# Stages of a graph attention kernel that end on a barrier of semaphores alone, with two stages' semaphores cleared together

## The reference

```python
for l in range(2):
    q, k, v = x @ Wq[l] + bq[l], x @ Wk[l] + bk[l], x @ Wv[l] + bv[l]     # each as (2500, 8, 64)
    a = (q[dst] * k[src]).sum(-1) * scale                                 # scores, (40000, 8)
    e = exp(a - segment_max(a, dst)[dst])
    alpha = e / (segment_sum(e, dst)[dst] + 1e-16)
    agg = segment_sum(alpha * v[src], dst)
    x = agg + (x @ Ws[l] + bs[l]) + enc
x = layer_norm(x)
x = layer_norm(relu(x @ W1 + b1) @ W2 + b2 + x)
return outer_layer_norm(x_in + x + enc)
```

## Time and profile before

| | us |
|---|---|
| median of 3 runs | 2167.22 |
| lowest and highest | 2167.22, 2171.39 |
| span of the profiled execution (first to last instruction) | 2163.2 |
| first collecting stage, start of its first VectorE operation | 566.59 |
| second collecting stage, the same | 1470.65 |
| start of `finish`, the same | 1889.98 |

### The profile page before, as it was taken

The page is one execution under the profiler, slowest core; times in us unless marked ns, Lnnn a source line. Parts: engine busy times, 40 slices in busy tenths (PEclk is TensorE's granted clock), DMA queues, the critical chain, the costliest instruction groups (busy, mean ns, idle before and its releaser), DMA issues. The chain is left out here.

```text
span 2163.2 us, 31856 instructions
## 1 busy us (share of the span) xinstructions
PE 1834.1 (85%) x7461; PEld 1388.8 (64%) x7462; DVE 1881.0 (87%) x2308; ACT 696.3 (32%) x1748; POOL 1447.3 (67%) x1428
## 2 busy tenths in 40 slices
PE   6778999998389999996899999974988877779997
PEld 5656666666267787774666666653766655557876
DVE  7659999999789999884899999996999988878894
ACT  3223333333265555552233333323111111132222
POOL 3067777777667777774677777775777777657653
PEclk9889999999599999998899999986999999979999
DMA  7589889888668888885788988885777777641111
GB/s 285 186 269 292 277 285 290 273 284 276 207 202 261 266 258 263 265 261 208 253 272 278 291 280 278 288 264 161 211 210 210 211 210 210 185 164 59 59 49 47
DMA packets 194709, 492.05 MB, mean 227 GB/s; under 512 B 36555, under 2 KB 57931, under 8 KB 194646
## 3 DMA queue, kind: packets, MB, share of 16 engines
q0 software_dynamic: 106624, 349.00, 52.9%
q1 hardware_dynamic: 85142, 137.07, 18.1%
q10 hardware_dynamic: 2880, 5.24, 0.7%
HBM read 431.21 MB, written 59.66 MB: 227 GB/s over the span
## 5 line engine op out<-in xcount | busy, mean ns | idle before, releaser
L845 POOL DMA_INDIRECT all_work<-k_rows,all_work x664 | 630.3, 949 | 227.1 <-issue 189.7
L845 POOL DMA_INDIRECT v_ring<-v_rows,coll_index x632 | 615.4, 974 | 215.5 <-issue 198.2
L1490 PE MATMUL coll_banks<-coll_ev,coll_hot 128*128 128x260 f32 x2656 | 646.9, 392 | 85.8 <-DVE coll_ev L1586 44.8
L1490 PEld LDWEIGHTS coll_banks<-coll_ev,coll_hot 128*128 128x128 f32 x2656 | 491.6, 192 | 220.8 <-DVE coll_ev L1586 104.5
L1048 PE MATMUL score_q_ps<-score_q,score_hot 128*128 x1328 | 394.3, 422 | 84.5 <-DVE score_q L1088 54.4
L1076 DVE TENSOR_TENSOR all_work<-score_q_ps,all_work 128x1024 f32<-128x1024 f32 x332 | 404.6, 1220 | 44.6 <-PE score_q_ps L1048 18.7
L1586 DVE TENSOR_TENSOR coll_ev<-v_ring,coll_banks 128x1024 f32<-128x1024 f32 x332 | 402.5, 1213 | 37.6 <-DMA v_ring<-v_rows,coll_index 32.2
L1081 DVE TENSOR_REDUCE graph_edge<-all_work 128x1024 f32 (+1 forms) x332 | 397.9, 1209 | 0.0
L1048 PEld LDWEIGHTS score_q_ps<-score_q,score_hot 128*128 128x128 f32 x1328 | 258.1, 200 | 177.7 <-issue 125.8
L1157 ACT ACTIVATE score_hot<-score_local,all_iota_col 128x512 fp32r<-128x512 uint8 x166 | 119.9, 723 | 589.8 <-DVE all_work L1076 557.0
L1600 DVE TENSOR_TENSOR all_work<-all_work,coll_banks 128x520 f32 x354 | 244.2, 690 | 25.7 <-PE coll_banks L1490 19.1
(11 more groups left out here) (312 smaller groups left out, 2348.9 us busy)
## 6 DMA issues: line engine op xcount, KB each, us to landing
score_xt<-x_turned SPq DMA_DIRECT2D x42, 512.0 KB, 5.9
all_work<-k_rows,all_work POOLq DMA_INDIRECT x664, 4.6
score_local<-local_dst SPq DMA_DIRECT2D x166, 64.0 KB, 6.0
x_turned<-keys_xt SPq DMA_DIRECT2D x20, 512.0 KB, 4.4
score_skip<-in_x SPq DMA_DIRECT2D x40, 256.0 KB, 4.8
v_rows<-score_v_out SPq DMA_DIRECT2D x40, 256.0 KB, 5.2
skip_rows<-score_skip SPq DMA_DIRECT2D x40, 256.0 KB, 3.8
x_turned<-coll_xt SPq DMA_DIRECT2D x20, 512.0 KB, 4.3
```

What stands on the lines that cost most here:

```text
L845: nc.gpsimd.indirect_dma_start(rows[:, slot, t, :], None, table, at).then_inc(arrived[slot], 16)
L1490: last = nc.tensor.matmul(sums[sum_slots[u]][:, part, :], m, ev[:, s % EVS, t, part * AGG // 2:(part + 1) * AGG // 2], start=s == 0 or t = ...
```

## The change

The blocks of `first_keys`, `score` and `soften_collect` are opened with `no_gpsimd_drain=True`. A block so opened retires the other four engines with their plain drains and ends on a barrier of semaphores, without the drain of GpSimd's queue. `build_constants` and `finish` keep the plain block. `score` no longer gives its semaphores back; it returns its phase, and `soften_collect` clears them together with its own in the first layer. In the second layer neither is cleared. The barriers inside `give_back` (line 111) stay plain.

```diff
-    def give_back(self):
-
-        self.nc.clear_and_free_semaphores(self.sems)
+    def give_back(self, *earlier):
+
+        self.nc.clear_and_free_semaphores([sem for ph in (self, *earlier) for sem in ph.sems])
         self.nc.all_engine_barrier()
...
-        with nc.Block() as block:
+        with nc.Block(no_gpsimd_drain=True) as block:
...
-        ph.give_back()
-
-
-def soften_collect(nc, k, layer):
+    return ph
+
+
+def soften_collect(nc, k, layer, scored):
...
-        if layer == 0:
-            ph.give_back()
+        if more:
+            ph.give_back(scored)
...
-                    score(nc, k, layer)
-                soften_collect(nc, k, layer)
+                    scored = score(nc, k, layer)
+                soften_collect(nc, k, layer, scored)
```

## The result

The changed kernel took 2158.59 us (median of 5 runs, 2156.07 to 2160.5), the kernel before beside it 2168.06 (5 runs, 2167.22 to 2171.39). The ratio is 0.996 with a 95% interval of 0.9947 to 0.9973. By the medians it is 9.5 us less, by the ends of the interval 5.9 to 11.5. The forecast was 2157.8 with a range of 2150 to 2164.

A forecast was written before the change was run, and what follows sets the result against it. No engine is full over the whole run; GpSimd's queue drain sets two of five stage ends. Gain 15.57 less 4.0 (table), 2.0 (returned drains) and 0.13 (clear) is 9.4 us: 2157.8 us, range 2150 to 2164.

The forecast's parts named there:

- The bottleneck and the sign: No engine is full over the whole run; GpSimd's queue drain sets two of five stage ends; faster, at 0.85.
- third rival: At the score ends, another wait replaces the drain until gathers have landed: 2167.9 us, no change; chance 0.09.
- Part one: Two score ends: without the drain VectorE starts the collecting stages earlier, 8.06 + 7.51 = 15.57 us gained.
- second rival: At the score ends, GpSimd's semaphore waits for the gathers' issue: gain 10.7 before costs, 2159.9 us; chance 0.13.
- Part two: Before the first scans, the `fresh` table lands 2.0 us later beside gathers in flight, twice: cost 4.0 us.
- fourth rival: Collecting stage starts: SyncE's table load falls far behind gathers, landing in 18.1 us: slower, 2182.2 us; chance 0.06.
- The first: Rival: the table before the first scan isn't slowed and returned drains take 40 ns: 15.4 us gained, 2151.8; chance 0.20.
- Part three: `give_back` after `first_keys` and the first collecting stage: returned full drains cost 1.0 us each, 2.0 in all.
- the worst case: Drains returned in `give_back` after `first_keys` and the first collecting stage cost 1.0 + 2.9 us, 3.9 in all.
- The joined clear: Clearing both stages' semaphores in one instruction: 24 more at some 5 ns each, cost 0.13 us.
- The sum: Whole kernel: 15.57 - 4.0 - 2.0 - 0.13 = 9.4 us gained, median 2157.8 us.
- The ring: Collecting stage: GpSimd's sixteen early gathers fill it before VectorE's first product; 10.1 us of standing still covers 1.5 us later gathers.

## Why the prediction was right, and where it was not

**The bottleneck and the sign** held. Two stage ends out of five were set by GpSimd's queue drain; without it both waits vanish. Putting GpSimd's drain back there, in the block (2168.01 us) or as a plain barrier behind it (2168.48), takes the whole gain away. That covers the third rival (a wait that takes the drain's place), which came out as an experiment and not as the change.

**Part one, 15.57 us**, measured 7.88 + 7.31 = 15.19. The semaphore signal ran ahead of the gathers (the barrier passed at 556.4, two gathers started at 556.96 and 558.55), as line 841 had let expect; the second rival is out. The starts come 0.49 us after the last reduction rather than the 0.32 that the sum used (0.04 to the end of VectorE's drain and 0.28 from there). The term was 0.4 too large. Its split held too: it gave some 0.7 us to each dropped `give_back`, and with the drain in place the profile has 0.6. With the drain gone, keeping them costs 2.6 to 3.1 us each, because their lesser drain waits for the issues (it ended 0.11 us behind the last one). The sum of 15.57 didn't depend on this.

**Part two, 4.0 us** for the later table, measured 1.74 + 2.34 = 4.1 in the profile of after. What delays it is settled: holding four gathers brings the landing back to 4.1 us, holding the `others` tables does not (6.4). The size is less certain than the agreement looks; it was taken from a load of 512 KB against one of 672. Over the four kernels whose code is the same at this point the idling was 1.70 to 3.87 us, 2.6 in the mean of eight, against 1.5 in the mean of six in kernels that drain: some 2.2 us for both stages. The landings were 4.3 to 6.5 us, which puts the fourth rival out (it needed over 10.6). The first (the table isn't slowed) is out too, though one stage with a landing of 4.3 and an idling of 1.70 came close to it.

**Part three, 2.0 us** for drains returned elsewhere, measured nothing: 45 ns where 40 had stood. This is the step that failed. It took 1.0 us from the drain at line 279, on the ground that the gathers had landed there, and passed over the lesser drain and the clear that stand in front of both returned drains. With these two in front a full drain took 45 ns even beside a gather in flight, so the landing isn't what makes it short. Where nothing stands in front, in `finish`, the returned drain took 6.6 us with all gathers landed, far more than the 1.0 charged and the 2.9 of the worst case. The prediction didn't count that place, and it was free only because VectorE ends later. The joined clear took 441 ns where the collecting stage's own had taken 313: 0.13 us, as worked out.

**The sum** of 9.4 us met a measured 9.5 in this comparison. That it met it so closely is luck, since it held a term of 2.0 us that wasn't there. With it at zero and the table at its mean the sum is 15.19 - 2.2 - 0.13 = 12.9 us; the four comparisons of kernels with this code at the score ends gave 9.5, 11.4, 11.2 and 10.2 us by their medians, so 1.5 to 3.4 us of that are still missing. They would have to lie in the steady loops, and these wander by more than that between executions of the same code (406.4 to 410.4 us from first product to next `score`, 450.5 to 455.2 for `score` of layer 1). The first of the two was 406.6 to 408.1 in the three profiles with full drains at the score ends' blocks and 408.8 in the mean of the nine that changed both ends, but 410.0 with the plain barrier's drains. So it isn't shown that the change lengthens the loop, and the missing part stays open. The ring was full at the first product, as predicted: GpSimd stood still 10.0 us before 595.4 and 11.0 before 1495.0.

**The profiled execution and the median.** The 4.0 us between the span of before and its median was taken for a fixed distance. It is 1.8 or 1.9 in every run that has both, so that profile was a quick execution of some 2165.0 us, with the shortest `finish` of all. The sum was applied to both span and median alike, so the forecast of the time didn't suffer, but that of the span did (2153.8 against 2158.7).

## What to carry to other kernels

A barrier that drains GpSimd's queue here cost 4.6 us or more behind the engine's last gather, on top of the 2 to 3 us by which GpSimd's issues ran past VectorE's work: about 8 us at a stage end. In these runs the cost stayed with the queue. The next full drain paid it also with the gathers landed for over 250 us (6.6 us, in `finish`), and took 45 ns where a lesser drain with a clear stood in front, so either take away all of them at a stage end or leave one where another engine hides it. Then look at what the earlier start runs into: here it was the first load of the next stage, and cutting that load to the part its first reader needs, with the transfers in its way held back as far as the next idle time of their issuer covers, was worth another 4 to 6 us. Before a difference between two profiles is explained, profile one of them again: a stage with unchanged code differed by 7.6 us between the two kernels and by 5.0 between two executions of one.

## What the runs showed of the hardware

- Three kinds of waiting on GpSimd's queue. A semaphore operation ran ahead of gathers that were still being issued (barrier at 556.4 us, two gathers started at 556.96 and 558.55). The lesser drain of a clear ended 0.11 us behind the last issue (2583 ns long). A full queue drain ended 4.6 to 6.7 us behind GpSimd's last issue or operation where 316 to 664 gathers were issued since the drain before, and 6.6 us behind it even with all of them landed for over 250 us (11294 ns).
- A full drain directly behind a lesser drain and a clear took 45 ns with a gather in flight, so it says nothing of landed data.
- A 672 KB load landed in 3.9 to 4.2 us where the gathers had drained or four of them were held (in the kernel before the DMA engines' share was 0.00 from 564 us to its issue at 566.46) and in 4.3 to 6.5 beside the last few gathers; 256 KB in 2.7 and 3.5 in the medians of the two cases, 0.8 later beside the gathers. How the DMA engines divide their time between the two no run here shows.
- A gather's issue took 0.95 us, and 5.48 where VectorE's third scan of 5.76 us (`coll_bwd` from `coll_fresh` and `coll_fwd`) lay beside it, 6.26 in the second layer. The kernel before has it too (5.51 us, at 577.45); over all profiles it was 5.26 to 6.43. It cost nothing, since the ring was full 10.0 us before it was needed:

```profile
568.12 0.95 POOL L845 DMA_INDIRECT v_ring<-v_rows,coll_index  x1 [0.31 <-issue]
569.38 5.48 POOL L845 DMA_INDIRECT v_ring<-v_rows,coll_index  x1 [0.30 <-issue]
```
